# Softmax sums on GpSimd, a router fed with raw tokens, and the first row maxima from full-precision matmuls

## The reference

```python
# layer 0: group norm (16 groups), 4 heads of 32 channels
qkv = einsum('bchw,oc->bohw', group_norm(x), qkv_weight)
attn = softmax(q.T @ k / sqrt(C), over the 1024 keys)
x = out_weight @ (attn @ v) + out_bias + x
t = tokens(x)                      # 1024 tokens of 128 per batch
# layer 1: linear attention, 8 heads of 16; K softmax over positions, Q over its 16 channels
t = t + Wr @ (context @ Q) + br    # of the layer norm of t
# mixture of experts, 8 experts, top 2; xt = layer_norm(t)
logits = xt @ Wr + br; top 2 of softmax(logits), weights renormalised
xn = layer_norm(xt) * ln_g[e] + ln_b[e]
t = t + sum over the two experts of w * (gelu(xn @ W1[e] + b1[e]) @ W2[e] + b2[e])
```

## Time and profile before

| | us |
|---|---|
| median of 3 runs | 394.5 |
| lowest, highest | 392.34, 397.24 |
| the profiled execution | 393.55 |
| its span | 391.8 |
| what lies around the span | 1.75 |

### The profile page before, as it was taken

One profiled execution on the slowest core, in us unless ns is written; L12 is line 12 of the kernel. 1 busy time (PEld: TensorE's weight loads), 2 busy tenths in 40 slices (PEclk: granted clock), 3 DMA queues, 4 the chain that ended last, 5 costly groups with the idle time before them and its releaser, 6 DMA issues.

```text
span 391.8 us, 6547 instructions
## 1 busy us (share of the span) xinstructions
PE 326.7 (83%) x1970; PEld 208.4 (53%) x1970; DVE 222.2 (57%) x693; ACT 187.9 (48%) x272; POOL 112.0 (29%) x142
## 2 busy tenths in 40 slices
PE   1766739998989989999999878198865998999985
PEld 1433323333433433544524254197865998999985
DVE  2446823456464556264655865376978566888610
ACT  1247115675656665465555511423370465777621
POOL 1086800000000000100011057500371777775420
PEclk9968556999999999999999999869697799999999
DMA  6069495535000000600000001120020214335124
GB/s 183 1 141 228 113 359 119 121 99 212 1 3 1 2 3 27 189 0 2 1 2 0 0 30 47 48 62 22 16 81 8 76 49 125 90 90 160 36 69 173
DMA packets 21773, 29.29 MB, mean 75 GB/s; under 512 B 4055, under 2 KB 15628, under 8 KB 21484
## 3 DMA queue, kind: packets, MB, share of 16 engines
q1 hardware_dynamic: 16828, 18.05, 17.0%
q0 software_dynamic: 3744, 10.31, 8.2%
q10 hardware_dynamic: 1168, 0.52, 0.5%
HBM read 11.62 MB, written 9.25 MB: 53 GB/s over the span
## 4 chain that ended last, share of the span: by engine, by line
PE 57%; DVE 18%; DMA 7%; POOL 7%; issue 6%; SPq 2%; ACT 1%; ACTq 0%; DVEq 0%; POOLq 0%
PE ps L794 13%; PE ps L989 8%; PE ps L977 8%; PE ps L757 6%; POOL expert_in L473 6%; PE ps L775 5%; DVE above L1081 4%; PE ps L737 3%; DMA Qs<-mrow 2%; SPq L331 2%; DMA Qs<-q_hi 2%; DVE pm L1084 2%; DMA attn<-in_L_conv_qkv_weight 1%; PE ps L859 1%; PE ps L693 1%
## 5 line engine op out<-in xcount | busy, mean ns | idle before, releaser
L536 ACT ACTIVATE probs<-ps 128x1024 f32<-128x1024 f32 x64 | 65.3, 1022 | 43.4 <-PE ps L775 43.4
L794 PE MATMUL ps<-probs,vT 128*32 128x512 f32 x256 | 69.2, 617 | 0.1
L794 PE MATMUL ps<-probs,ones 128*32 128x512 f32 x256 | 69.2, 617 | 0.0
L1081 DVE CUSTOM_DVE_ANT_0 above<-ps,above 128x512 f32<-128x512 f32 x56 | 38.7, 691 | 50.3 <-PE ps L757 49.0
L416 POOL TENSOR_TENSOR rstd<-ve,minus_half 128x8 f32<-128x8 f32 (+1 forms) x8 | 11.1, 1385 | 191.5 <-DVE ve L1120 175.2
L989 PE MATMUL ps<-w,GT 128*128 x368 | 52.8, 289 | 7.9 <-ACT GT L637 7.3
L637 ACT ACTIVATE GT<-H 128x512 f32<-128x512 f32 x46 | 29.0, 631 | 57.4 <-DVE H L1342 57.2
L989 PEld LDWEIGHTS ps<-w,GT 128*128 128x128 f32 x368 | 48.0, 204 | 9.6 <-issue 9.5
L977 PE MATMUL ps<-XTT,w1s 128*128 128x128 f32 x368 | 52.4, 289 | 0.0
L529 ACT ACTIVATE above<-ps 128x512 f32<-128x512 f32 x56 | 33.5, 599 | 38.5 <-PE ps L737 38.5
L478 POOL DMA_INDIRECT token_out<-Y,yidx x46 | 44.1, 959 | 22.1 <-DVE Y L1353 14.3
(11 more groups left out here) (185 smaller groups left out, 426.1 us busy)
## 6 DMA issues: line engine op xcount, KB each, us to landing
expert_in<-zeros POOLq DMA_DIRECT2D x2, 1495.0 KB, 8.1
...
```

The costliest lines, as they stand in the source:

```text
L536: nc.scalar.activation(probs[:, s % 3, :], bank(2 + 2 * (s % 2), 2), ACT.Exp).then_inc(exp_done, 1)
L794: last = nc.tensor.matmul(bank(6 + o % 2)[i * HD:(i + 1) * HD, :], w, probs[:, s % 3, hd * HALF:(hd + 1) * HALF], start=kt == 0, stop=kt = ...
L1081: nc.vector.tensor_tensor_reduce(above[:, n % 2, :], bank(base), above[:, n % 2, :], scale=1.0, scalar=-3.0e38, op0=ALU.add, op1=ALU.max, ...
```

## The change

**Sums.** `values` now computes only v: four matmuls of 256 columns, in the four column groups (two heads, two halves of the queries). The exp blocks are added by POOL, four steps (a "quad") into one block with three additions of 128x1024 (`add_probs`); `sums_of` multiplies ones with the two quad sums of a product, two steps after it began to be complete. Of the last quad only one addition is made, and PE takes the other two blocks itself. The exp buffers are five (NPR); an exp waits until values and addition of the step five before are done, and the exp of step 3 waits for the stacks of units 0 and 1, whose sources the new buffers overlie. POOL starts the additions behind the zeroing DMAs of expert_in and its wait for them. Three rsqrts are placed between additions (NORMS_AT).

**Router.** The router's weights are centred once (`centre`: one matmul and one DVE instruction). tokenT transposes the raw t2 and logits come from it; the row's rstd multiplies them afterwards. The parts move to earlier steps, norm2 goes to ACT as eight instructions behind a small DVE one (`shift`).

**First eight maxima.** Slots 0 to 7 now alternate between the heads, and come from full-precision matmuls over the 32 rows of a head in q32 and k32, copies that ACT makes of PSUM; no stack is needed. They run ahead of the projections of batch 1, and so does the first rows slot, whose two DMAs ACT issues. ACT copies x into XP (L588) ahead of batch 1's split, DVE norms batch 1 after slots 0 and 1. The zeroing of expert_in waits until these row maxima have landed (before: until they were computed).

The diff, cut to its core (left out: semaphores, names, the centring, a wait on x2_ready in the tokens of batch 1):

```diff
+    NPR = 5
+    QUADS = UNITS * 2 * L // P // 4
+    QSPAN = 256
...
+        q32, k32 = probs[:, 0, :], probs[:, 1, :]
...
-        order = [(k, i) for k in range(2 * UNITS) for i in range(RING - 1)]
-        for k in range(2 * UNITS):
+        order = [(0, QH * hd + t) for t in range(QH) for hd in range(2)]
+        order += [(k, i) for k in range(1, 2 * UNITS) for i in range(RING - 1)]
+        order.insert(PLAIN_FIRST, (0, "rows"))
+        for k in range(1, 2 * UNITS):
...
-            return (6, 7) if g < AHEAD and g % 2 else (0, 1)
+            if g < PLAIN_FIRST:
+                return ((4, 5), (2, 3), (6, 7), (0, 1))[g % 4]
+            return (6, 7) if g == PLAIN_FIRST or g < AHEAD and g % 2 else (0, 1)
...
-        LAYER1_AT = {BEGIN_LAYER1: "residual", 34: "project", 35: "tokens_stats tokens", 39: "keys",
+        LAYER1_AT = {BEGIN_LAYER1: "centre residual", 35: "project", 36: "tokens_stats tokens", 39: "keys",
                      40: "keys_exp", 41: "query_value0", 42: "query_value1", 44: "keyT", 45: "queries_exp",
                      46: "queries queries_scaled context", 47: "fold", 48: "queryT", 49: "queryT_sb",
-                     50: "attend stats", 52: "norm stats2", 54: "tokenT", 55: "tokenT_sb", 56: "logits",
-                     57: "gates_exp", 58: "route choose", 60: "counts norm2"}
+                     50: "attend stats", 51: "tokenT", 52: "tokenT_sb norm", 53: "logits stats2",
+                     54: "gates_exp", 55: "shift route choose", 56: "norm2", 57: "counts"}
         LAYER1_AT_TILE = {"before": "residual project tokens_stats tokens keys keys_exp query_value0 query_value1 "
                                     "keyT queries_exp",
                           0: "queries queries_scaled context", 1: "fold", 2: "queryT queryT_sb", 3: "attend stats",
-                          4: "norm", 5: "stats2 tokenT", 6: "tokenT_sb", 7: "logits", 8: "gates_exp",
-                          9: "route choose counts norm2"}
+                          4: "tokenT tokenT_sb norm", 5: "logits stats2", 6: "gates_exp", 7: "shift route choose norm2",
+                          8: "counts"}
...
+        NORMS_AT = {(8, 3): 0, (12, 2): 1, (13, 1): 2}
+        LAST_QUAD = UNITS * STEPS - 4
+        def added_by(s):
+            return 3 * (s // 4) + max(1, s % 4) if s < LAST_QUAD + 2 else 3 * (QUADS - 1) + 1
+        def query_span(o, i):
+            return bank(6 + o % 2)[64 * i:64 * i + 64, 0:QSPAN]
...
-            pool.wait_ge(mhl_ready, 1)
+            pool.wait_ge(mrow_in[0], 16 * 2)
...
+            def add_probs(q, i):
+                s = 4 * q + i
+                pool.wait_ge(exp_done, s + 1)
+                if i == 1 and q >= 3:
+                    pool.wait_ge(sum_done, (q - 3) // 2 + 1)
+                if i > 1:
+                    pool.wait_ge(probs_added, added_by(s - 1))
+                nc.gpsimd.tensor_tensor(quad_sum(q), probs_of(s - 1) if i == 1 else quad_sum(q), probs_of(s),
+                                        ALU.add).then_inc(probs_added, 1)
+            row_numbers(0)
+            pool.wait_ge(resid_ready, B)
+            for q in range(QUADS):
+                for i in range(1, 4 if q < QUADS - 1 else 2):
+                    add_probs(q, i)
+                    if (q, i) in NORMS_AT:
+                        rsqrt(B + NORMS_AT[q, i])
...
-            rsqrt(B)
-            rsqrt(B + 1)
-            rsqrt(B + 2)
             scatter(0, lambda j: rsqrt(B + 3) if j == 3 else None)
+            pool.wait_ge(sum_done, 2 * UNITS)
+            row_numbers(1)
...
+                last = nc.scalar.activation(q_hi[b][:, :], bank(4, 2), ACT.Copy, scale=SCORE_SCALE)
+                if b == 0:
+                    last = nc.scalar.activation(q32, bank(4, 2), ACT.Copy, scale=SCORE_SCALE)
...
-                if s >= 3:
-                    act.wait_ge(pv_done, s - 2)
-                nc.scalar.activation(probs[:, s % 3, :], bank(2 + 2 * (s % 2), 2), ACT.Exp).then_inc(exp_done, 1)
+                if s == 3:
+                    act.wait_ge(stack_in[0], 16 * (6 + SP_LOADS))
+                    act.wait_ge(stack_in_pool, 16 * (6 - SP_LOADS))
+                    act.wait_ge(stack_in[1], 16 * 12)
+                if s >= NPR:
+                    act.wait_ge(pv_done, s - NPR + 1)
+                    act.wait_ge(probs_added, added_by(s - NPR))
+                nc.scalar.activation(probs_of(s), bank(2 + 2 * (s % 2), 2), ACT.Exp).then_inc(exp_done, 1)
...
+            def a_norm2(b):
+                act.wait_ge(nm2_ready, b + 1)
+                for j in range(J):
+                    last = nc.scalar.activation(X2[:, b, j, 0:D], F[:, j, :], ACT.Identity, bias=nm2[:, b, j:j + 1],
+                                                scale=rstd[:, B + 3 * b + 2, j:j + 1])
+                last.then_inc(x2_ready, 1)
...
+            act.wait_ge(mrow_ready, 1)
+            for hd in range(2):
+                dst = Qs[SPLIT:STACK, 0, head(0, hd), 0:HALF]
+                act.dma_start(dst.bitcast(f32).rearrange("s (t q) -> s t q", t=QH),
+                              mrow[hd * 2 * QH:(hd + 1) * 2 * QH, :].bitcast(f32)).then_inc(mrow_in[0], 16)
             split(1)
...
-                        pe.wait_ge(qk_split, i + 1)
-                        if i:
-                            pe.wait_ge(kd_made, b)
+                        pe.wait_ge(slot_used, PLAIN_FIRST + i)
...
+            def max_tile(t):
+                g = 2 * t
+                if t == 0:
+                    pe.wait_ge(hi_ready, 2)
+                    pe.wait_ge(qk_split, 1)
+                    pe.wait_ge(v_sb, 1)
+                elif t == 1:
+                    pe.wait_ge(qk_split, 2)
+                    pe.wait_ge(kd_made, 1)
+                    pe.wait_ge(wT_sb, 2)
+                    pe.wait_ge(vcol_sb, 2)
+                else:
+                    pe.wait_ge(slot_used, g - 2)
+                for h in range(2):
+                    for hd in range(2):
+                        r = slice(HD * head(0, hd), HD * head(0, hd) + HD)
+                        last = nc.tensor.matmul(bank(slot_banks(g + hd)[h]), q32[r, t * P:(t + 1) * P],
+                                                k32[r, h * HALF:(h + 1) * HALF], start=True, stop=True)
+                        if h:
+                            last.then_inc(slot_ready, 1)
...
-                for i, w in ((hd, vT[:, b, kt, n * HD:(n + 1) * HD]), (2 + hd, ones[:, 0:HD])):
-                    last = nc.tensor.matmul(bank(6 + o % 2)[i * HD:(i + 1) * HD, :], w,
-                                            probs[:, s % 3, hd * HALF:(hd + 1) * HALF],
-                                            start=kt == 0, stop=kt == KT - 1)
...
+            def values(s):
+                u, step = s // STEPS, s % STEPS
+                b, kt = u // PAIRS, step % KT
+                o = s // KT
+                pe.wait_ge(exp_done, s + 1)
+                if kt == 0:
+                    if o >= 2:
+                        pe.wait_ge(o_used, o - 1)
+                    else:
+                        pe.wait_ge(slot_used, AHEAD)
+                for i in range(2):
+                    for hd in range(2):
+                        n = head(u, hd)
+                        last = nc.tensor.matmul(query_span(o, i)[hd * HD:(hd + 1) * HD, :],
+                                                vT[:, b, kt, n * HD:(n + 1) * HD],
+                                                probs_of(s)[:, hd * HALF + i * QSPAN:hd * HALF + (i + 1) * QSPAN],
+                                                start=kt == 0, stop=kt == KT - 1)
+                last.then_inc(pv_done, 1)
+            def sums_of(o):
+                parts = [quad_sum(2 * o), quad_sum(2 * o + 1)]
+                if o < 2 * UNITS - 1:
+                    pe.wait_ge(probs_added, added_by(KT * o + KT - 1))
+                else:
+                    pe.wait_ge(probs_added, added_by(LAST_QUAD))
+                    parts += [probs_of(LAST_QUAD + 2), probs_of(LAST_QUAD + 3)]
+                if o >= 2:
+                    pe.wait_ge(o_used, o - 1)
+                for n, part in enumerate(parts):
+                    for i in range(2):
+                        for hd in range(2):
+                            r = (2 * i + hd) * HD
+                            last = nc.tensor.matmul(bank(6 + o % 2)[r:r + HD, QSPAN:2 * QSPAN], ones[:, 0:HD],
+                                                    part[:, hd * HALF + i * QSPAN:hd * HALF + (i + 1) * QSPAN],
+                                                    start=n == 0, stop=n == len(parts) - 1)
+                last.then_inc(sum_done, 1)
...
-                pe.wait_ge(n2_ready, b + 1)
+                pe.wait_ge(t2_ready, b + 1)
                 for j in range(J):
-                    last = nc.tensor.transpose(ps[:, j * P:(j + 1) * P], F[:, j, :], ident[:, :])
+                    last = nc.tensor.transpose(ps[:, j * P:(j + 1) * P], t2[:, b, j, :], ident[:, :])
...
+            for t in range(QH):
```

(37 more changed lines are left out.)

101 lines of the change are left out of this document (57 added, 44 removed).

## The result

The median after is 434.12 us (4 runs, 430.57 to 443.23) against 395.87 (4 runs) for the kernel before on the same chip: ratio 1.095, 95% interval 1.083 to 1.107. The run of 443.23 had the lowest granted clock of the four and stands outside the ratio. The forecast was 386 with a range of 374 to 404, so the direction and the range were both wrong.

What follows compares the result with a forecast made beforehand. TensorE was read as busiest: 83% of the 391.8 us span, 57% of the chain. Terms +0.6 - 3.8 - 1.7 - 2.3 + 2.0 - 3.3 = -8.5 gave 385.0 from 393.55, 386 from the median; own range 380 to 391, with rivals 374 to 404.

Steps and rivals of the forecast that it cites:

- Term 1: Start to exp of step 5: early first score is lost waiting for GpSimd; +0.6 us (-1.2 to +3.4).
- Term 2: Steps 5 to 33: sums on GpSimd, values with half the columns; -3.8 us (-9.5 to +8).
- the allowance of "+3" for the lock: Within Term 2: short DVE instructions wait for a running GpSimd addition at seven places; +3 us (0 to +15).
- the gain without the lock: Within Term 2: two-maxima steps -7.5 us, one-maximum steps -2, three closings +2.7.
- Term 3: Steps 33 to 49: GpSimd becomes the bound with 35.5 us; 39 us for 40.7, -1.7 (-5.2 to +4).
- Term 4: Steps 50 to first scatter: shorter chain, GpSimd additions before the scatter; 30.7 us for 33.0, -2.3 (-6.3 to +4).
- The scatter's pause: First scatter pauses after six transfers for batch 1's rsqrt; +2 us (0 to +3).
- batch 1 between tiles: Batch 1's routing between expert tiles moves earlier, its scatter at about 299.5 for 302.8; -3.3 us (-5 to 0).
- A: Rival: DVE's short instructions slip between additions, so parts 2 to 4 gain fully; -23.5, 374 us with gaps; chance 0.20.
- C: Rival, first maxima: heads in two row groups run in turn, or PE at half clock; +5, 391 us; chance 0.12.
- B: Rival: DVE instructions with SBUF operands wait for additions in rows slots, norm and routing; 404 us, slower; chance 0.20.

Runs made afterwards that it cites:

- pe_sums: Kernel after with the softmax sums back on PE and no GpSimd additions: 388.31 us, 0.988 of the kernel before; repeated on the third chip 412.28 us, 0.983.
- thin_pe: `pe_sums` with the ones' matmuls in only one of eight steps, seven eighths of the sums left out: 380.00 us profiled, 388.74 in the other run.
- run 7: Kernel after, each rows slot's two 8-element DVE instructions replaced by one reduction, split remainder left out, additions kept: 443.72 us, 1.060 of the kernel before.
- no_lock_max: The same run as run 7: kernel after without the waiting DVE instructions in the rows slots, 443.72 us, 1.060 of the kernel before.
- half_add: Kernel after with each GpSimd addition cut to 128x512, the second head's sums left out: 439.16 us, 1.051 of the kernel before on its chip.

## Why the prediction was wrong

*Term 1, the start:* right in time. Forecast 72 to 77, middle 74; measured 72.6. The first score starts at 50.21 ("near 50"), and GpSimd's iota behind the zeroing starts at 69.68 (range 69 to 74). The early maxima are stored in front of GpSimd as described; `pe_sums`, which has no addition to wait for, reaches exp 5 at 64.0. What the term left out is what its wait does to the steps behind it: PE stands for 5.90 us, the clock falls to 0.50, and steps 6 to 9 take 13.1 us, 2.5 more than before and 3.7 more than in `thin_pe`.

*Term 2, steps 5 to 33:* the step that failed is the allowance of "+3" for the lock, with the sentence that "half falls beside the row slot". The mechanism stood in the text (seven places, 2.20 for 0.17 us), and with no stop a step of two maxima does take 2.59 (forecast 2.62). The sum of the waits was about right too: 6.6 us forecast for seven places, 7.5 measured in the six of this stage. Wrong were three things. First, a wait in the rows slot isn't hidden: PE's banks are free only after it (run 7), and the three steps with a stop take 8.9 us more than before. Second, two of the three stops are followed by steps of up to 3.88 at the lower clock, +5.9 in all; the forecast priced an idle PE at its idle time, though it had rows at both clocks before it. Third, the gain without the lock, -9.5 + 2.7 = -6.8, was over-counted: `thin_pe`, where nothing waits for an addition, takes 77.8, 3.4 us less than before. Its clock falls in two places, with steps of up to 3.88 us there for the usual 2.59. Measured +14.2 against -3.8.

*Term 3, steps 33 to 49:* PE's packed steps are shorter, as forecast (1.23 us for 1.66). What failed is that "this engine becomes the bound", GpSimd with 35.5, and the norm's waits as a small addition to it. GpSimd was busy for 32.1 of 52.6 us, so it was no bound; one norm between two PE phases was, with 6.1 us of waits and the low clock behind it. Steps 41 and 35 alone cost +10.8 and +3.0, of which `pe_sums`, without additions, has +1.7 and +0.8.

*Term 4, step 50 to the scatter:* the shortening of the chain is real, 8.1 us with the sums on PE (24.9 for 33.0). With the additions it costs 11.5: a norm that waits twice, four waits of about 2 us, PE and the exps stopped behind them, GpSimd idle in turn, and the scatter behind the last additions. The forecast's 30.7 was 26.7 of GpSimd's work and "four for PE's stop at the counts and for DVE held up"; the four should have been 44.6 - 26.7 = 17.9, and GpSimd's four longest idle times in this stage do add up to 17.5 us.

*The scatter's pause and batch 1 between tiles:* +2.0 and -3.3, -1.3 in sum; measured +0.8 and -0.6 with the dense tail, +0.2 in sum. About right, and small.

*The rivals.* A, the lock hardly bites: false, though most of the rows slots' products did take 0.17 us. C, row groups one after the other: false (the first two tiles together took 3.70 us); its other half, the low clock, came for the last tile (3.78 us), and the first rows slot's products were done at 35.9, so nothing was lost by it. B was the mechanism, with its places, and even its count of three additions inside the norm was exact; it was given 0.20 and priced at 404 instead of 434. Two arguments had held it down: that one memset row was thin evidence, and that short instructions slip between the additions. They do: eight of the twelve in the rows slots did not wait, nor did five of the eight of the norm. But a few waits on the chain were enough, and B, like the forecast, put no price on the clock behind a stop.

The rule that B leaned on, in the Trainium skill, "SBUF — State Buffer", Who interferes with whom, is borne out in each part that runs here touch: a DVE product from SBUF waits until the GpSimd instruction that is running ends (2.19 for 0.17 us), one with two SBUF inputs too (2.30), a reduction did not in any of eight places (161 to 163 ns). Its sentence that "PE and ACT never wait on anyone" holds for the port and misleads for the time: PE stood for 2.1 and 8.7 us behind the DVE instructions that waited.

**What stays open.** When the clock falls behind a PE pause. The pause's length alone does not decide it: with the same values of 256 columns it fell behind pauses of 1.27 and 1.28 us (after, `thin_pe`, `no_lock_max`) and stayed at 1.00 behind 1.29 (`half_add`) and 2.10 (after, before 114.28). Nor is it shown why the clock came back after 7 us in the kernel after and after 20 in `no_lock_max`. For the two later stages the waits are read from the chain, and only `pe_sums` and `half_add` bear on them; no run took single waits away there, as `no_lock_max` does for the rows slots. And why the second and third chip take 24 us more behind the first scatter: single pauses of 2 to 12 us stand there, which the profile puts down to "remote", and none stands in the profiles of the first chip.
